# A graph layer's weighted scatter: runs of ten edges added up on VectorE before the products on TensorE

## The reference, cut to what matters

```python
h   = relu(layernorm(x))
m   = concat([h[src], h[dst], edge_attr_32])              # 64 + 64 + 32 columns
msg = silu(m @ W1 + b1) @ W2 + b2
att = softmax(silu(m @ Wa1 + ba1) @ Wa2 + ba2, axis=0)    # over all edges
agg = segment_sum(msg * att, dst)                         # one row of 64 per node
out = x + silu(concat([h, agg]) @ Wu1 + bu1) @ Wu2 + bu2
```

## Time and profile before

| | |
|---|---|
| median of 3 runs | 2105.85 us |
| profiled execution, span (no other time is recorded for it) | 2482.0 us |
| POOL busy | 1529.9 us, 62% |
| PE busy, DVE busy, ACT busy | 1101.1, 1086.6, 919.5 us |
| POOL idle put down to DVE L911 and L912 | 354.2 and 22.2 us |
| PE idle put down to "issue", L622 and L636 | 963.8 and 274.8 us |
| DVE's largest one-off rows in the groups | L850, L851: 1.8 us each; L1015: 3.4 us |

### The profile page before, as it was taken

How to read it: one execution, slowest core, us unless ns; L and a number is a source line. 1 busy time by engine, 2 the same in 40 slices (tenths; PEclk the granted TensorE clock), 3 DMA queues, 4 the chain that set the end, 5 groups by cost and what they waited for, 6 DMA issues and landing times.

```text
span 2482.0 us, 21022 instructions
## 1 busy us (share of the span) xinstructions
PE 1101.1 (44%) x6767; PEld 963.4 (39%) x6767; DVE 1086.6 (44%) x2367; ACT 919.5 (37%) x1107; POOL 1529.9 (62%) x1628
## 2 busy tenths in 40 slices
PE   4334444444444444444444444444444444444447
PEld 3223343444333333444333334343433333444444
DVE  4344444444444444444444444444444444444445
ACT  3333333334333333334333333343433333333433
POOL 4666666666666666666666666666666666666650
PEclk8566666666666666666666666666666666666766
DMA  7433333333333333333333333333333333333321
GB/s 202 106 90 90 90 89 88 92 91 95 98 93 88 90 88 88 90 93 90 99 95 89 89 90 89 87 94 89 98 95 91 89 90 90 87 93 90 95 65 27
DMA packets 101990, 228.43 MB, mean 92 GB/s; under 512 B 45184, under 2 KB 65460, under 8 KB 91636
## 3 DMA queue, kind: packets, MB, share of 16 engines
q1 hardware_dynamic: 47588, 120.63, 18.5%
q0 software_dynamic: 51584, 105.75, 17.2%
q10 hardware_dynamic: 2704, 0.66, 0.1%
HBM read 218.91 MB, written 8.00 MB: 91 GB/s over the span
## 4 chain that ended last, share of the span: by engine, by line
issue 48%; PE 33%; DVE 9%; another core or an unknown queue 7%; ACT 1%; SPq 1%; DVEq 0%; DMA 0%; ACTq 0%
PE bank L622 20%; PE bank L636 11%; DVE hot L865 2%; DVE v L902 2%; DVE bank L912 1%; DVE prod L895 1%; PE bank L732 1%; PE bank L722 0%; DVE lgb L921 0%; DVEq L875 0%; ACT comb L492 0%; PE bank L584 0%; ACT s L524 0%; PE bank L655 0%
## 5 line engine op out<-in xcount | busy, mean ns | idle before, releaser
L404 POOL DMA_INDIRECT p_rows<-p_tab,src_all x1612 | 1521.9, 944 | 872.3 <-issue 464.7
L622 PE MATMUL bank<-q_win,comb 128*128 128x128 f32 x3224 | 723.7, 369 | 981.9 <-issue 963.8
L622 PEld LDWEIGHTS bank<-q_win,comb 128*128 128x128 f32 x3224 | 643.9, 279 | 1099.1 <-issue 1095.4
L492 ACT ACTIVATE comb<-dst_b,row_of 96x1024 f32<-96x1024 int32 (+1 forms) x162 | 219.0, 1352 | 1336.6 <-PE bank L622 1227.8
L911 DVE TENSOR_TENSOR bank<-bank,p_rows 128x128 f32<-128x128 f32 x80 | 23.9, 299 | 1205.5 <-remote 672.6
L636 PE MATMUL bank<-hot,v 128*65 128x96 f32 x3200 | 320.1, 252 | 344.7 <-issue 274.8
L636 PEld LDWEIGHTS bank<-hot,v 128*65 128x65 f32 x3200 | 282.7, 141 | 342.1 <-issue 264.5
L912 DVE TENSOR_TENSOR bank<-bank,p_rows 128x512 f32<-128x512 f32 (+1 forms) x403 | 266.5, 666 | 71.7 <-PE bank L622 38.6
L524 ACT ACTIVATE s<-bank 128x512 f32<-128x512 f32 x403 | 232.1, 589 | 108.7 <-DVE bank L912 83.8
L498 ACT ACTIVATE comb<-comb,ones 96x1024 f32<-96x1024 f32 (+1 forms) x162 | 218.9, 1351 | 2.7
L865 DVE TENSOR_TENSOR hot<-bank,rel 128x960 f32<-128x960 f32 x162 | 178.3, 1139 | 0.0
(11 more groups left out here) (108 smaller groups left out, 304.0 us busy)
## 6 DMA issues: line engine op xcount, KB each, us to landing
dst_b<-dst_row SPq DMA_DIRECT2D x80, 960.0 KB
p_rows<-p_tab,src_all POOLq DMA_INDIRECT x1612
comb<-efT SPq DMA_DIRECT2D x80, 320.0 KB
q_win<-q_tab SPq DMA_DIRECT2D x81, 48.0 KB
p_tab<-s SPq DMA_DIRECT2D x12, 256.0 KB
q_tab<-s SPq DMA_DIRECT2D x12, 256.0 KB
out<-s SPq DMA_DIRECT2D x6, 256.0 KB, 2.3
x_sb<-x SPq DMA_DIRECT2D x2, 512.0 KB, 5.1
```

Source lines behind the costliest of these rows:

```text
L404: pool.indirect_dma_start(p_rows[:, a, t * H2:(t + 1) * H2], None, p_tab, bass.IndirectOffsetOnAxis(src_all[:, g * TG + t:g * TG + t + 1], ...
L492: nc.scalar.activation(comb[0:WIN, a, c0:c1], dst_b[:, c0:c1], ACT.Abs, bias=row_of[0:WIN, bass.ds(g, 1)]).then_inc(abs_ok, 1)
L622: last = nc.tensor.matmul(ps_z[q][:, (t % TQ) * H2:(t % TQ + 1) * H2], comb[:, a, t * P:(t + 1) * P], q_win[:, a, :], start=True, stop=True)
```

## The change

**Layout of the edges.** In a full group, partition p now holds 20 consecutive edges, where tile t held 128 consecutive edges before. The host lays out `src`, `dst`, `dst_row` and `efT` accordingly, in the same shapes. `dst` is sorted, so the ten edges of a half row (a run) belong to few nodes.

**Sums.** In groups 0 to 78 DVE splits each run in two segments: edges with the node of the run's first edge, and the rest, which must all have the node of its last edge. It adds each segment up (`segment_sums`), so that PE has four products per group (two runs by two segments) in place of 20, and the one-hots shrink from 20 x 96 to 4 x 96 columns (`run_hots`). Groups 79 and 80 keep a product per tile. The input has no node with fewer than 15 edges, so a run of ten never touches three nodes.

**Check.** `worst_fit()` also tests that each run fits, and keeps the mask `first_run` (128 x 1612) for all groups.

```diff
-    edges = np.concatenate([np.arange(full), np.arange(N_EDGES - last, N_EDGES)])
+    edges = np.concatenate([np.arange(full).reshape(-1, P, EDGE_TILES).transpose(0, 2, 1).reshape(-1),
+                            np.arange(N_EDGES - last, N_EDGES).reshape(P, -1).T.reshape(-1)])
...
             def sums(g):
-                pe.wait_ge(v_ok, g + 1)
-                pe.wait_ge(hot_ok, 2 * g + 2)
+                pe.wait_ge(hot_ok, hots_ready(g))
                 wait(pe, acc_ok, g)
+                if by_tile(g):
+                    pe.wait_ge(v_ok, LAST + g)
+                else:
+                    pe.wait_ge(run_ok, 2 * g + 2)
...
-                for t in range(T):
-                    last = nc.tensor.matmul(ps_part[0:U1, 0:WIN], v[:, t, :], hot[:, t * WIN:(t + 1) * WIN], start=(t == 0), stop=(t == T - 1))
+                n = products(g)
+                for i in range(n):
+                    what = v[:, i, :] if by_tile(g) else run_sum[:, i, :]
+                    last = nc.tensor.matmul(ps_part[0:U1, 0:WIN], what, hot[:, i * WIN:(i + 1) * WIN], start=(i == 0), stop=(i == n - 1))
...
 # worst_fit, after the reductions that it had
+                for lo, hi, n in ((0, LAST * TG, TG // RUNS), (LAST * TG, C // P, TL // RUNS)):
+                    of_run = rel[:, lo:hi].rearrange("p (r t) -> p r t", t=n)
+                    for keep, end in ((first_run, 0), (fits, n - 1)):
+                        nc.vector.tensor_tensor(keep[:, lo:hi].rearrange("p (r t) -> p r t", t=n), of_run,
+                                                of_run[:, :, end:end + 1].broadcast_to([P, (hi - lo) // n, n]), ALU.is_equal).then_inc(run_fit, 1)
+                dve.wait_ge(run_fit, 4)
+                chain(nc.vector.tensor_tensor(fits[:], fits[:], first_run[:], ALU.max))
+                chain(nc.vector.tensor_reduce(bad[:, 0:1], fits[:], AX.X, ALU.min))
...
+            def run_hots(g):
+                n = tiles(g) // RUNS
+                nc.vector.tensor_tensor(hot[:, 0:SEGS * WIN].rearrange("p (r k n) -> p r k n", r=RUNS, k=2),
+                                        iota_c[:, 0:WIN].unsqueeze(1).unsqueeze(1).broadcast_to([P, RUNS, 2, WIN]),
+                                        runs(rel, g)[:, :, 0::n - 1].unsqueeze(3).broadcast_to([P, RUNS, 2, WIN]), ALU.is_equal).then_inc(hot_ok, 1)
...
+            def segment_sums(g, a):
+                T = tiles(g)
+                n = T // RUNS
+                here = slice(g * TG, g * TG + T)
+                weighed = [vs[:, k, 0:T * U1].rearrange("p (r u t) -> p r u t", r=RUNS, u=U1) for k in range(2)]
+                nc.vector.tensor_tensor(w_run[:, 0, 0:T], ps_w[:, 0:T], first_run[:, here], ALU.mult).then_inc(w_run_ok, 1)
+                nc.vector.scalar_tensor_tensor(w_run[:, 1, 0:T], first_run[:, here], 0.5, ps_w[:, 0:T], ALU.is_lt, ALU.mult).then_inc(w_run_ok, 1)
+                for k in range(2):
+                    dve.wait_ge(w_run_ok, 2 * g + 1 + k)
+                    nc.vector.tensor_tensor(weighed[k].rearrange("p r u t -> p r t u"), s2[:, a, 0:T, 0:U1].rearrange("p (r t) u -> p r t u", r=RUNS),
+                                            w_run[:, k, 0:T].rearrange("p (r t) -> p r t", r=RUNS).unsqueeze(3).broadcast_to([P, RUNS, n, U1]), ALU.mult).then_inc(v_ok, 1)
+                for k in range(2):
+                    dve.wait_ge(v_ok, 2 * g + 1 + k)
+                    nc.vector.tensor_reduce(run_sum[:, k::2, :], weighed[k], AX.X, ALU.add).then_inc(run_ok, 1)
```

More of the change, by code:

```diff
@@ L56, in build @@
     RING = 6
+    RUNS = 2
+    SEGS = 2 * RUNS
     ACT_ODD = 6
     assert NT == NB * NBT + 1 and NT == UB * UT + 1 and NG % 2 == 1 and NB == 12
-    assert 0 <= DUP < P and TL % TQ == 0 and TL > 2 * TQ and src.shape == (P, C // P)
+    assert 0 <= DUP < P and TL % TQ == 0 and TL > 2 * TQ and TG % RUNS == 0 and TL % RUNS == 0 and src.shape == (P, C // P)
     assert H2 == P and 2 * D == P and U == D and DE * TQ == P
@@ L126, in build @@
         p_rows = sb("p_rows", [P, 2, TG * H2])
+        first_run = sb("first_run", [P, C // P])
         hot = sb("hot", [P, TG * WIN])
+        run_sum = sb("run_sum", [P, SEGS, U1])
         comb = sb("comb", [P, 2, TG * P])
@@ L139, in build @@
         fade = sb("fade", [P, 2])
-        v = sb("v", [P, TG, U1])
+        vs = sb("vs", [P, 2, TG * U1])
         acc = sb("acc", [U1, NP])
@@ L145, in build @@
         rz = sb("rz", [P, 1])
+        v = vs[:, 0].rearrange("p (t u) -> p t u", u=U1)
+        fits = flat(vs)[:, 0:C // P]
         s2_all = s2[:].rearrange("p a t u -> p (a t u)")
@@ L162, in build @@
         ps_w = ps_small[:, 2 * P:2 * P + TG]
+        w_run = ps_small[:, 3 * P:3 * P + 2 * TG].rearrange("p (k t) -> p k t", k=2)
         iota_c = bank[7][:, 0:P]
@@ L190, in build @@
             sem(n) for n in ("z_done", "z_ok", "silu_ok", "s_ok", "lg_ok", "qmax_ok", "qmaxB_ok", "top_ok", "negm_ok"))
-        (w_ok, wm_ok, v_ok, part_done, acc_ok, ref_ok) = (
-            sem(n) for n in ("w_ok", "wm_ok", "v_ok", "part_done", "acc_ok", "ref_ok"))
-        (bad_ok, misfit_ok, flag_ok) = (sem(n) for n in ("bad_ok", "misfit_ok", "flag_ok"))
+        (w_ok, wm_ok, w_run_ok, v_ok, run_ok, part_done, acc_ok, ref_ok) = (
+            sem(n) for n in ("w_ok", "wm_ok", "w_run_ok", "v_ok", "run_ok", "part_done", "acc_ok", "ref_ok"))
+        (run_fit, bad_ok, misfit_ok, flag_ok) = (sem(n) for n in ("run_fit", "bad_ok", "misfit_ok", "flag_ok"))
         (ws_ok, zp_ok, refx_ok, scaled_ok, zall_done, zall_ok, rz_ok) = (
@@ L257, in tiles, with by_tile, products, hots_ready @@
             return TL if is_last(g) else TG
+        def by_tile(g):
+            return g >= LAST - 1
+        def products(g):
+            return tiles(g) if by_tile(g) else SEGS
+        def hots_ready(g):
+            return g + 1 + max(0, g + 2 - LAST)
+        def runs(t, g):
+            return t[:, g * TG:g * TG + tiles(g)].rearrange("p (r t) -> p r t", r=RUNS)
         def per(a, g, n):
@@ L665, in _ @@
             pe.wait_ge(acc_ok, LAST)
-            pe.wait_ge(v_ok, NG)
+            pe.wait_ge(v_ok, 2 * LAST)
             for t in range(TL):
                 if t in (0, TL // 2):
-                    pe.wait_ge(hot_ok, 2 * LAST + 1 + 2 * t // TL)
+                    pe.wait_ge(hot_ok, hots_ready(LAST) - 1 + 2 * t // TL)
                 if t == TL // 2 + 2:
@@ L683, in group_any @@
                     for q in range(T // TQ):
-                        wait(pe, g_zok, g * NQ + q - 1)
+                        wait(pe, g_th, g * NQ + q - 1)
                         pe.sem_inc(turn, 1)
@@ L852, in worst_fit @@
                 chain(nc.vector.tensor_scalar(bad[:, 0:1], bad[:, 0:1], float(1 - WIN), None, ALU.add))
-                nc.vector.scalar_tensor_tensor(bad[:, 2:3], bad[:, 1:2], -1.0, bad[:, 0:1], ALU.mult, ALU.max).then_inc(bad_ok, 1)
+                chain(nc.vector.scalar_tensor_tensor(bad[:, 2:3], bad[:, 1:2], -1.0, bad[:, 0:1], ALU.mult, ALU.max))
+                for lo, hi, n in ((0, LAST * TG, TG // RUNS), (LAST * TG, C // P, TL // RUNS)):
[6 more added lines that the diff above has]
+                chain(nc.vector.tensor_reduce(bad[:, 0:1], fits[:], AX.X, ALU.min))
+                chain(nc.vector.tensor_scalar(bad[:, 0:1], bad[:, 0:1], -1.0, 1.0, ALU.mult, ALU.add))
+                nc.vector.tensor_tensor(bad[:, 2:3], bad[:, 2:3], bad[:, 0:1], ALU.max).then_inc(bad_ok, 1)
             def set_flag():
@@ L859, in set_flag, with tile_hots @@
                 nc.vector.tensor_scalar(flag[:], bad1[:, 2:3], 0.0, None, ALU.is_gt).then_inc(flag_ok, 1)
-            def one_hots(g, k):
+            def tile_hots(g, k):
                 T = tiles(g)
@@ L950, in weighted @@
                 dve.wait_ge(w_ok, 2 * g + 2)
-                weigh(T, a, a).then_inc(v_ok, 1)
+                if by_tile(g):
+                    weigh(T, a, a).then_inc(v_ok, 1)
+                else:
+                    nc.vector.tensor_reduce(wsum[:, a:a + 1], ps_w[:, 0:T], AX.X, ALU.add)
+                    segment_sums(g, a)
             def group(g, a):
@@ L972, in group @@
                 if late:
-                    one_hots(g - 1, 0)
-                    one_hots(g - 1, 1)
+                    run_hots(g - 1)
                     weighted(g - 1, 1 - a)
@@ L990, in last_group @@
                 add_part(g - 2, a)
-                one_hots(g - 1, 0)
-                one_hots(g - 1, 1)
+                tile_hots(g - 1, 0)
+                tile_hots(g - 1, 1)
                 weighted(g - 1, 1 - a)
@@ L1022, in _ @@
             add_part(LAST - 1, 1, node_before)
-            one_hots(LAST, 0)
+            tile_hots(LAST, 0)
             dve.wait_ge(ref_ok, 2 * LAST)
@@ L1029, in _ @@
             nc.vector.tensor_tensor(v[:, 0:TL, :], s2[:, 0, 0:TL, 0:U1], ps_w[:, 0:TL].unsqueeze(2).broadcast_to([P, TL, U1]), ALU.mult).then_inc(v_ok, 1)
-            one_hots(LAST, 1)
+            tile_hots(LAST, 1)
```

5 lines of the change are left out of this document (2 added, 3 removed).

## The result

The changed kernel takes 2109.07 us (median of 20 runs, 2103.58 to 2112.55); the kernel before took 2105.87 us beside it (20 runs, 2101.06 to 2108.49). The ratio is 1.0017, 95% interval 1.0009 to 1.0025: 0.17% slower, inside the 0.2% of "no change", though the interval leaves out 1, so a small slowdown is real. Forecast were 2108.9 us and 1.0014. The profiled execution of the changed kernel has a span of 2110.4 us and was timed at 2112.11.

The account below looks back on a forecast made before the run. POOL's gather rhythm of 1.248 us was taken to bound the timed runs. The sum was 2105.85 + 0 (TensorE) + 0 (VectorE, last groups, layout) + 3.0 (check) = 2108.9 us, 0.14% slower, range 2102 to 2115.

Parts of the forecast that it names:

- What bounds the kernel: Whole run: POOL's gather rhythm of 1.248 us sets the timed runs; the other engines have room in each 24.96 us group.
- these stretches: TensorE's slow passes behind POOL's 351.8 us of pauses, taken as belonging to the profiled execution alone.
- The sum of a timed run: Kernel before: profile without pauses 2131.2 us, less 30.6 of tail, gives 2100.6; 5.2 us to the median lie around the span.
- TensorE: Groups 0 to 78 lose 16 of 20 products each; worth 0 in timed runs, since POOL does not wait for PE.
- VectorE in the groups: 79 groups: net +3.1 us each, to 15.9 of 24.96 us, products at 1.49; hidden under the gathers, costs 0.
- The check: Longer worst_fit(), once: three long VectorE instructions with two SBUF inputs hold gathers up 1.0 us each, 3.0 us in all.
- The rival: Segment sums in the groups: strided products of 6.0 us or more make DVE the bound, 2264 us at 7.0; chance 0.03.
- bound from below: Check: with the worst-timed start each long instruction holds a gather 0.45 us (1.82 - 1.25 - 0.12), in all 1.3.
- upper bound of 5.5 us: Check: the three long instructions hold POOL for their whole length, 5.5 us.
- the slower rival: Check costs more: 5.5 us, or up to 8 if gathers hold DVE, add_rows(1, 0) is late and the tail adds 2; chance 0.22.
- The last groups: Groups 79 and 80: quarters 3 and 4 wait behind 3.1 us more DVE work; costs 0, up to 2 us if late.
- Signs: Changed kernel's profile: pauses under 30 us, span 2100 to 2140, two to four long gathers at 105 to 125 us, products 1.5 us.

Follow-up runs that it names:

- e11: Kernel before, with the sums of groups 0 to 78 taken over only the first 4 of 20 tiles: 2107.86 us, ratio 1.0002.
- e3: Changed kernel plus 20 extra 128x1600 VectorE instructions in groups 10 to 29, both inputs in SBUF: 2138.96 us, ratio 1.0148.
- e5: Changed kernel with products written contiguously and reductions reading with the stride: 2521.81 us, ratio 1.0154 to a kernel before of 2483.82 us.
- e10: Changed kernel with four more segment-sum products per group on VectorE: 2796.55 us, ratio 1.123 to a kernel before of 2490.94 us.
- e8: Kernel before, sums of groups 0 to 78 over only the first 4 of 20 tiles: 2436.77 us, ratio 0.9802 to a kernel before of 2483.82 us.
- e9: The changed kernel itself, unaltered, beside a kernel before of 2490.94 us: 2503.75 us, ratio 1.0051.
- e2: Changed kernel with the check's long instructions and the subtraction at the start each having an input in PSUM: 2107.81 us, ratio 0.9998.
- e1: Changed kernel with run ends copied to PSUM and masks joined there, so no long check instruction has two SBUF inputs: 2107.47 us, ratio 1.0001.
- e4: Changed kernel plus 20 extra 128x1600 VectorE instructions in groups 10 to 29, second input in PSUM: 2111.17 us, ratio 1.0021.
- e6: Changed kernel with two more segment-sum products per group on VectorE: 2518.44 us, ratio 1.0154 to a kernel before of 2483.82 us.

## Why the prediction was right, point by point

**What bounds the kernel.** The conclusion held, the reason given for it did not. POOL's step of 1.248 us sets the runs near 2106 us: no pause is left in the profile after, e11 takes TensorE's work away for nothing, and e3 adds the gathers' losses one for one. But "I take these stretches for something of the profiled execution alone" is false. The profiles of e5 to e10 have them, and timed runs beside these took as long as such a profile: the kernel before 2484 and 2491 us, next to the 2482.0 us of its own. That the first profile came from such a chip while the 2105.85 us came from others fits, but no run here shows it. On a chip of the other kind the same arguments would have given a wrong time: there TensorE's relief alone is worth 2.0% (e8), which the whole change does not bring (e9 and e5, ratios 1.005 and 1.015). The forecast of the time also needed the runs of the result to meet a chip like that of the 3 runs before (2105.85 us), which nothing in the prediction could know: that much is luck.

**The sum of a timed run.** 2100.6 us and 5.2 around it should read some 2104 and 1.7 around it (2112.11 - 2110.4). The closest profile to a timed run of the kernel before is e11's: 45.7 + 2013.2 + 0.95 + 47.1 = 2107.0 us (the last is 2107.0 less the others). Against the estimate its head is 5.7 us longer, its gathers 2.0 and its tail 1.4 shorter. The first gather starts anywhere from 39.1 (e2) to 45.7 us (the changed kernel and e11), which the estimate took at 40.0; so part of the 5.2 us was in the head. The changed kernel's tail came out at 48.1 us, against 48.5 (79.1 - 30.6), and the landing at 2.5 us against 2.7. That the median came within 0.2 us of the forecast is in part luck: the interval of the ratio allows 1.9 to 5.3 us for the change.

**TensorE.** 0 was right (e11). The passes of the sums are 632 and 40, as said.

**VectorE in the groups.** 0 was right, the term in it was too small: a product takes 2.455 us and not 1.49, and the load came out at 17.4 us and not 15.9. The step that failed is the choice of L902 and of the memset of 40 elements for a strided write; it cost nothing because the load is hidden. e5 shows that the stride is the cause, at some 0.75 ns per element. The rival fell, since 6.0 us for a product was needed. The Trainium skill ("SBUF — State Buffer", section "Door 1: The DMA port swizzle") says that accesses which go on to a new 16-byte line pay. These runs agree in direction; none has a stride that stays within such a line, so the line length itself is not tested.

**The check.** 3.0 us was forecast, 2.67 measured in the gathers, and its mechanism is shown by the traces of e1 to e4 and by the times of e3 and e4. Each of the three instructions holds one gather, for 1.38, 0.50 and 0.79 us where the sum had 1.0 for each; their sum came close because the errors cancel. What sets the hold is where the gather begins: it lasts for what is left of the VectorE instruction, less some 0.12 us, as in the prediction's bound from below. The upper bound of 5.5 us would need gathers that begin with the instructions. VectorE is not held by gathers (its instructions took 1.83, 1.82 and 1.84 us, and 1.82 in e1), and `add_rows(1, 0)` at 97.94 us was no pause for POOL, so what the slower rival added to 5.5 us did not come. What the Trainium skill ("SBUF — State Buffer", section "Who interferes with whom") says of two SBUF inputs and of one holds here (e3 against e4), and the gather is the one that waits.

**The last groups.** 0 was right, with 1.51 us to spare.

**Signs.** Pauses under 30 us and a span of 2100 to 2140 came true, but not for the reason given. The 29 runs of the kernel before beside e1 to e4 have spans of 2091.7 to 2109.8 us without any change, so it is not TensorE's relief that shortened the profile from 2482.0 us. The three long gathers came as forecast in number and length, but at 90.5 to 96.6 us and not at 105 to 125, since the groups start earlier without slow stretches (`add_rows(1, 0)` at 97.94 us, against 115.81). The products took 2.46 us and not 1.5, and VectorE's busy time was put at 1340 us and was 1455.

## What to carry to other kernels

Look first for the engine whose steps are evenly spaced and have no releaser: here 1612 gathers at 1.248 us, and VectorE, the busiest of the others in its groups, had 7.6 us per group to spare. Then ask of each new instruction not how long it is but what it takes from that engine: three instructions with both inputs in SBUF took 2.67 us from it, and 158 strided products with 158 reductions nothing that the profile shows. Putting one operand in PSUM costs a short copy and frees the gathers. And when the profile's span and the timed median are hundreds of us apart, do not assume that the profile is the odd one out: look for timed runs as long as the profile. A sum that fits one of them does not tell why the other differs.

## What the runs showed of the hardware that was not expected

- The same kernel took 2107 and 2108 us on two chips and 2484 and 2491 us on two others, 18% more. Each chip was met once, so whether this belongs to the chip or to its condition at that time is not shown. In the slower profiles TensorE's and VectorE's instructions come at multiples of about 0.70 us, mostly for 16 to 23 us at a time, while POOL keeps its step (701 steps within such stretches of the first profile are 1.248 us long on average). Fewer TensorE products shorten the time there (e8, 2484 to 2437 us), and the whole change does not (e9). More load on VectorE alone did not lengthen it: e6, with some 5 us more per group than e5, took 2518 us against 2522. What paces the instructions was not found.
- A gather that begins during a VectorE instruction with two SBUF inputs ends 0.81 to 0.83 us after that instruction, whatever its own start (the 20 of e3 and the 3 of the check); one that began 0.04 us before it is not touched.
- A VectorE instruction over 1300 fp32 elements takes 1.48 to 1.50 us contiguous and 2.44 to 2.47 us with a stride of 40 bytes written or 260 bytes read.
- The first gather starts at 45.7 us in the changed kernel's profile and at 42.0 in the same kernel's e9, which is more than the check takes from the gathers. The distance of first and last gather is freer of that, but its ordinary step also moved between 1.2485 and 1.2502 us among the unpaused profiles (e3 and e1), 2.7 us over 1611 steps.
